# One program of Mamba, experts, attention and grouped experts: the last norm, routing, grouped experts and output woven into the attention turns

## The chip, the cores and the metric

The kernel runs on one core of one Trainium2 chip. The time is device microseconds of a whole execution, the median of three runs. The engines are PE (TensorE), DVE (VectorE), ACT (ScalarE), POOL (GpSimd) and SP, which here only issues transfers.

## The reference, cut to what matters

Two transformer-like layers on x of 8 batches x 512 tokens x 128 features, fp32. The first layer (a bidirectional Mamba block and a top-1 expert block) is the same in both kernels. The second layer is what the change touches:

```python
h = _layernorm(x) * (1 + ca) + sa                       # second norm
x = x + ga * attention(h)                               # 16 heads of 8, causal, rotary
h = _layernorm(x) * (1 + cb) + sb                       # third norm
x = x + gb * moe(h)
# moe: 16 experts of width 64 in 4 groups; scores = sigmoid(h @ router.T); the 2 best groups,
# the 4 best experts in them, weights scaled to 2.5; and 2 shared experts of width 64
#   combine = [tokens, 16]; y = sum_e combine[t,e] * (silu(h@gate_e.T) * (h@up_e.T)) @ down_e.T + shared
```

No batch of this part needs another batch, so the norm, the routing and the experts of a batch may run as soon as its attention is done.

## The kernel before, in words

Data lie transposed: `xT` and `hT` hold 128 features on the partitions and 8 x 512 tokens along them. The program is a row of stages, each an `nc.Block()` whose five engine programs meet at its end: setup, norm, Mamba (L391 to L579), norm, routing, experts, norm, **attention** (L991 on), third **norm** (`layernorm_stage`, L197 to L273), **group routing** (`group_route_stage`, which also computes silu(gate)*up of the first two batches, L1494 and L1587), **grouped experts** (`group_experts_stage`) and **output** (`output_stage`). All but the last five are alike in both kernels.

Attention works in **turns**, one per batch t, and a turn in eight **slots**, 2 to 9. A slot treats one pair of heads:

- *scores*: five PSUM banks of keys x queries (`pe_scores`, L1125, mask added by a second product, L1126), each followed by ACT's exponential (L1222) into `PT`. In slots 8 and 9 they are already those of the next turn.
- *values* in every even slot: 16 narrow fp32 products of four heads (`pe_values`, L1155), then ACT copies the bank out (L1253), PE transposes it (`G0` to `G3`, L1104) and DVE divides (L1303, L1305).
- *maxima* of the next turn: 44 banks (L1140, L1141) per turn, each reduced by DVE (L1270), in slots 2 to 8; after each half DVE splits the 32 columns of negated maxima into three bf16 parts (L1277 to L1285), PE transposes them (`MA`, `MB`) and they go through DRAM into the query stack.
- *projections* of turn t+2: `q`, `q_swap`, `k`, `k_swap` (L1098) in slots 2 to 5, DVE's rotation (L1297), POOL's sum and residues (L1338 to L1342), ACT's bf16 casts (L1231). SP stores these parts and loads them back as a stack (`store_parts`, `load_stack`, L1350 to L1357). PE waits for the stack of turn t+1 before the maxima in slot 2.
- at the turn's end `F` (transpose, L1111) and `O` (output projection, L1113), each waited for by the next, and DVE's update of `xT` (L1317).

`psM` and `psS` (maxima and scores) have three PSUM banks each, `psO` and `mb` one; all one-off products go through `mb` in a fixed order. The order of PE's and DVE's work within a slot is written by `slot_items` and `pe_turn`; three passes of a loop hold turns 0 to 5. An **experts chunk** (nine per batch, eight routed and one shared) is G (gate), silu on ACT, U (up), a multiplication by DVE, C (the routing weights spread over the expert's rows), a second multiplication, D (down); here every one of the banks `psG`, `psU`, `psC`, `psY` is double.

Of the kernel before, what the change touches and what calls it, by code (L numbers as in the profile page):

```python
# [990 lines left out]
def attention_stage(nc, W, W3, tiles, scratch_q, scratch_k, m_scratch, hT, xT, identb, gate):  # L991
# [15 lines left out]
    BEFORE, EACH = 11, 13  # L1007
    with ExitStack() as ctx:
# [49 lines left out]

        def uses(more_p, more_m):

            order = [x for slot in SLOTS_T for x in EARLY.get(slot, []) + LATE.get(slot, [])] + TAIL
            kept = [x for x in order if (more_p or x[0] not in "qk") and (more_m or x not in ("V", "MA", "MB"))]
            return {x: n for n, x in enumerate(kept)}

        def slot_items(c, slot):
# [9 lines left out]
            return items + [x for x in LATE.get(slot, []) if x in c.use]  # L1075

        class Turn:
            def __init__(self, t, p, base, more_p=True, more_m=True):
                self.t, self.p, self.base, self.more_p, self.more_m = t, p, base, more_p, more_m
                self.use = uses(more_p, more_m)  # L1080

        def turns(eng, body):

            with eng.Fori(0, 3) as i:
                for p in range(2):
                    body(Turn(2 * i + p, p, BEFORE + EACH * (2 * i + p)))
            at = BEFORE + EACH * 6
            last = Turn(6, 0, at, more_p=False)
            body(last)
            body(Turn(7, 1, at + len(last.use), more_p=False, more_m=False))  # L1090
# [761 lines left out]
```

## Time and profile before

| | us |
|---|---|
| runs: 2150.10, 2152.92, 2160.95; median | 2152.92 |
| the profiled execution, its own time | 2167.51 |
| its span | 2165.8 |
| from the start of attention (1317.0) to the end of the span | 848.8 |
| of it attention | 552.5 |
| third norm | 27.7 |
| group routing, with gate and up of two batches | 62.9 |
| grouped experts | 194.4 |
| output | 11.3 |
| busy in the whole span: PE, DVE, ACT, POOL | 1745.6, 1434.5, 992.8, 906.7 |

The stretches are counted from the span's start. An engine's busy time is a union of its instructions and tells little alone: within a turn the question is which engine the others wait for. Matmul records overlap, so the distance from one start to the next is the cost of a product, not its length. An fp32 product of 512 columns is recorded as two matmuls.

### The profile page before, as it was taken

The page shows a single profiled execution, that of the slowest core. Times are in us where ns is not written, and L with a number is a line of the kernel's source. Part 1 is how long each engine was busy: PE and PEld are TensorE (multiplying, and loading weights), DVE is VectorE, ACT ScalarE, POOL GpSimd, SP SyncE. Part 2 cuts the span into 40 slices and gives each one's busy share as a digit, 9 for nine tenths or more (in the row PEclk, how much of TensorE's full clock was granted, in tenths as well). Part 3 has the DMA queues.
Part 4 walks back from the last instruction along what each step waited for, and adds up shares of the span by engine and source line. Part 5 has one row for each costly group of instructions (what it writes and reads, how often), then busy time and mean ns, then how long its engine had stood idle before and what let it go on. Part 6 is the DMA issues. An engine that isn't in the chain of part 4 may idle for free. (4 is left out here: it accounts for less than half of the span.)

```text
span 2165.8 us, 24099 instructions
## 1 busy us (share of the span) xinstructions
PE 1745.6 (81%) x7317; PEld 854.3 (39%) x7317; DVE 1434.5 (66%) x1594; ACT 992.8 (46%) x1553; POOL 906.7 (42%) x507
## 2 busy tenths in 40 slices
PE   7788888888888898877838746878777788888998
PEld 5233333333333333332537633434443445543333
DVE  3099999999999999999432122656555556274444
ACT  3566666666656666663203322244343344441111
POOL 1277777777777777776250143011110010040000
PEclk8889999999999999999959955599898898987999
DMA  3112122212121222121014213221123220100001
GB/s 133 40 59 78 60 78 78 74 62 78 78 76 61 78 78 77 59 79 58 16 39 113 86 36 81 69 75 47 32 75 77 76 70 8 44 1 0 0 0 39
DMA packets 49081, 128.25 MB, mean 59 GB/s; under 512 B 5478, under 2 KB 36046, under 8 KB 39094
## 3 DMA queue, kind: packets, MB, share of 16 engines
q1 hardware_dynamic: 45782, 117.65, 17.0%
q0 software_dynamic: 3216, 9.51, 1.3%
q8 instruction: 50, 0.82, 0.2%
q14 instruction: 33, 0.27, 0.0%
HBM read 104.04 MB, written 23.01 MB: 59 GB/s over the span
## 5 line engine op out<-in xcount | busy, mean ns | idle before, releaser
L535 POOL TENSOR_TENSOR PR<-H,CS 128x1024 f32<-128x1024 f32 x256 | 601.9, 2356 | 202.5 <-DVE H L510 192.2
L510 DVE TENSOR_TENSOR_SCAN H<-DA,X 128x1024 f32<-128x1024 f32 x256 | 583.5, 2280 | 0.2
L433 PE MATMUL psY<-PR,W 128*128 128x512 f32 x1024 | 486.8, 598 | 1.1 <-POOL PR L535 1.1
L496 ACT ACTIVATE DA<-DT,negA 128x511 f32<-128x511 f32 x512 | 332.0, 711 | 96.0 <-DVE H L510 95.6
L503 DVE TENSOR_TENSOR X<-DU,psB 128x1024 f32<-128x1024 f32 x256 | 314.5, 1229 | 68.9 <-POOL DU L554 36.6
L433 PEld LDWEIGHTS psY<-PR,W 128*128 128x128 f32 x1024 | 193.7, 192 | 229.7 <-issue 215.2
L1222 ACT ACTIVATE a_PT<-a_psS 128x512 f32<-128x512 f32 x320 | 181.3, 601 | 156.5 <-PE a_psS L1126 152.9
L1270 DVE TENSOR_REDUCE a_MX<-a_psM 128x1 f32<-128x384 f32 (+3 forms) x352 | 206.8, 637 | 60.9 <-PE a_psM L1141 59.5
L413 PE MATMUL psB<-ST,sel 96*128 96x512 bf16 x256 | 100.4, 392 | 143.7 <-DVE X L503 143.6
L1140 PE MATMUL a_psM<-a_kst,a_qst 72*128 72x512 bf16 (+3 forms) x512 | 147.5, 336 | 35.1 <-DMA a_kst<-scratch_k 22.8
L1125 PE MATMUL a_psS<-a_qst,a_kst 75*128 75x512 bf16 (+3 forms) x512 | 138.4, 319 | 18.3 <-issue 17.0
L413 PEld LDWEIGHTS psB<-ST,sel 96*128 96x128 bf16 x256 | 24.7, 96 | 300.9 <-DVE X L503 289.7
L391 PE MATMUL pp<-work,convW 128*128 (+1 forms) x256 | 123.0, 605 | 4.0 <-ACT pre L457 1.4
L1338 POOL TENSOR_TENSOR work<-work 128x512 f32<-128x512 f32 x16 | 20.2, 1264 | 231.0 <-DVE work L1297 231.0
L1141 PE MATMUL a_psM<-a_mqk,identb 128*128 128x128 bf16 x512 | 111.0, 242 | 0.0
L1297 DVE TENSOR_TENSOR work<-a_mb,work 128x512 f32<-128x512 f32 x32 | 22.1, 692 | 125.9 <-PE a_mb L1098 125.8
L1652 ACT ACTIVATE f_SG<-f_psG 128x512 f32<-128x512 f32 x54 | 32.2, 597 | 159.2 <-PE f_psG L1625 159.2
L1126 PE MATMUL a_psS<-a_mkq,identb 128*128 128x128 bf16 x512 | 101.6, 230 | 0.0
L1155 PE MATMUL a_psO<-a_PT,a_VA 128*32 128x512 f32 (+3 forms) x1024 | 98.5, 482 | 2.4 <-issue 1.6
L1140 PEld LDWEIGHTS a_psM<-a_kst,a_qst 72*128 72x128 bf16 x512 | 54.5, 107 | 104.1 <-DVE a_MX L1270 49.1
L1587 POOL TENSOR_TENSOR HE<-g_SG,g_UC 128x512 f32<-128x512 f32 x18 | 23.5, 1308 | 153.1 <-ACT g_UC L1516 153.1
L1253 ACT COPY a_OT<-a_psO 128x512 f32<-128x512 f32 x32 | 18.7, 585 | 145.7 <-PE a_psO L1155 145.7
(252 smaller groups left out, 2539.5 us busy)
## 6 DMA issues: line engine op xcount, KB each, us to landing
CS<-c_rows SPq DMA_DIRECT2D x64, 1024.0 KB, 4.6
scratch_q<-a_partsq SPq DMA_DIRECT2D x24, 384.0 KB, 3.6
a_qst<-scratch_q SPq DMA_DIRECT2D x8, 1152.0 KB
a_kst<-scratch_k SPq DMA_DIRECT2D x24, 384.0 KB
scratch_k<-a_partsk SPq DMA_DIRECT2D x8, 384.0 KB, 5.9
slots<-zeros POOLq DMA_DIRECT2D x1, 2624.0 KB, 10.1
stok<-slots SPq DMA_DIRECT2D x3, 768.0 KB, 7.2
work<-in_pack SPq DMA_DIRECT2D x1, 2272.0 KB, 9.6
```

Of the source, the lines that this page charges most:

```text
L391: last = nc.tensor.matmul(pp[:, :], convW[:, tap, n * P:(n + 1) * P], XP[:, ds((of + 1) * XW + tap, T)], start=tap == 0, stop=tap == KC - 1)
L413: nc.tensor.matmul(psB[:, :], sel[:, s, :], ST[p][:, :], start=True, stop=True).then_inc(B_ready, 1)
L433: last = nc.tensor.matmul(chunk(psY, c), w("ident"), chunk(PR[n % 4], c), start=False, stop=n == NS - 1)
L496: last = nc.scalar.activation(DA[:, s % 4, c, 1:T], chunk(DT[p], c)[:, 1:T], ACT.Exp, scale=negA[:, c * NS + s:c * NS + s + 1])
L503: nc.vector.tensor_tensor(both(X[s % 2][:, :]), both(DU[p][:, :]), psB[:, :].unsqueeze(1).to_broadcast([P, NCH, T]), ALU.mult).then_inc(mu ...
L510: nc.vector.tensor_tensor_scan(H[s % 4][:, :], DA[:, s % 4, :, :].rearrange("p c t -> p (c t)"), X[s % 2][:, :], 0.0, ALU.mult, ALU.add).t ...
L535: nc.gpsimd.tensor_tensor(both(PR[s % 4][:, :]), both(H[s % 4][:, :]), CS[q % 2][:, s % 4, :].unsqueeze(1).to_broadcast([P, NCH, T]), ALU. ...
L1125: nc.tensor.matmul(out, kst[p][:, at + i * P:at + (i + 1) * P], qst[p][:, at + i * P:at + T], start=True, stop=False)
L1140: nc.tensor.matmul(out, qst[p][0:72, at + j * P:at + (j + 1) * P], kst[p][0:72, at:at + wide], start=True, stop=False)
L1141: last = nc.tensor.matmul(out[:, j * P:wide], identb[:, :], mqk[:, :], start=False, stop=True)
L1222: nc.scalar.activation(PT[k % 4][u][:, :], psS[S_BUF[5 * k + u]][:, :], ACT.Exp, scale=DK ** -0.5).then_inc(E_done, 1)
L1270: nc.vector.tensor_reduce(MX[:, j, h0:h0 + nh], src, AX.X, ALU.max).then_inc(M_used, 1)
```

## The change

`attention_stage` takes over the last norm, the routing and the experts of six batches; `last_experts_stage` does the rest. The stages third norm, group routing, grouped experts and output are gone.

- Turn t does, beside its attention: `F` and `O` of batch t-1 (now in slot 2), its norm (`XC`, `VR`, `RB`), logits (`LG`) and routing (51 small DVE operations in slots 6, 7, 8: `GroupRoute`), the transposed weights (`CP`, slot 9); for t >= 2 the nine chunks of batch t-2, one per slot and two in slot 9; for t >= 3 the last down product, the update of `xT` and the transposes and store (`OUT`) of batch t-3 in slot 2.
- One PSUM bank `psE` takes G, U and C of a chunk in turn, `psY` the down products. For them `psM` and `psS` have two banks where they had three.
- Silu is 0.5x * (1 + tanh(0.5x)): ACT writes 0.5x into `GH` and tanh into `TH`, POOL multiplies and adds. (Silu's own table is used in the last stage only.)
- The masks of a scores bank are added in one product; `HB` is gone; the exponentials' buffers `PT` fall from four sets to three; loops are unrolled. The weights of the experts (`W4`) are loaded in the attention prologue behind the second stack.
- `last_experts_stage`: norm and routing of batch 7 among the 18 chunks of batches 6 and 7, with double banks and silu on ACT; the outputs of both.

```diff
-        psM = [ps(f"psM{i}") for i in range(3)]
-        psS = [ps(f"psS{i}") for i in range(3)]
-        psO, mb = ps("psO"), ps("mb")
+        psM = [ps("psM0"), ps("psM1")]
+        psS = [ps("psS0"), ps("psS1")]
+        psO, mb, psE, psY = ps("psO"), ps("mb"), ps("psE"), ps("psY")
...
-        LATE = {3: ["G0"], 4: ["V"], 6: ["MA"]}
-        TAIL = ["F", "O"]
+        LATE = {2: ["XC", "OUT"], 3: ["G0", "VR"], 4: ["V", "RB"], 5: ["LG"], 6: ["MA"], 9: ["CP"]}
+        LEAD = ["F", "O"]
+        ROUTE_SLOTS = {6: ((0.3, 0), (0.8, 1)), 7: ((0.3, 2), (0.8, 3)), 8: ((0.3, 4), (0.8, 5))}
+        CHUNKS = {slot: (slot - 2,) if slot < 9 else (7, 8) for slot in SLOTS_T}
...
+        def slot_plan(t, slot):
...
+                add([("S", t + ahead, slot - PAIRS * ahead, u) for u in range(5)], 0, 0.55 if slot % 2 == 0 else 0.9)
+            if slot % 2 == 0:
+                add([("V", t, slot // 2 - 1, i) for i in range(QT)], 0.55, 1)
...
+            add(items, 0.6 if slot == 2 else 0, 1)
+            add([("mb", t, x) for x in LATE.get(slot, []) if wanted(t, x)], 0.93, 1.02)
...
+                if slot < 9:
+                    plan += [(0.03, ("G", n)), (0.62, ("U", n)), (0.88, ("C", n))]
+                else:
+                    plan += [(0.03, ("G", n)), (0.35, ("U", n)), (0.5, ("C", n)), (0.55, ("G", n + 1)), (0.7, ("D", n)), (0.95, ("U", n + 1))]
+                if n % 9:
+                    plan.append((0.15, ("D", n - 1)))
+            if slot == 2 and t >= 1:
+                plan += [(0.15, ("mb", t, "F")), (0.4, ("mb", t, "O"))]
+                if t >= 3:
+                    plan += [(0.25, ("D", 9 * (t - 3) + 8)), (0.5, ("moe", t - 3))]
+            return [tag for _, tag in sorted(plan, key=lambda x: x[0])]
...
+            if what == "G":
...
+                elif c == 0:
+                    pe.wait_ge(HU_done, n)
+                else:
+                    pe.wait_ge(HC_done, RC * b + c)
+                nc.tensor.matmul(psE[:, :], w4("gate_w")[:, c * P:(c + 1) * P], h, start=True, stop=True).then_inc(G_ready, 1)
+            elif what == "U":
+                pe.wait_ge(TH_ready, n + 1)
+                nc.tensor.matmul(psE[:, :], w4("up_w")[:, c * P:(c + 1) * P], h, start=True, stop=True).then_inc(U_ready, 1)
+            elif what == "C":
+                pe.wait_ge(HU_done, n + 1)
...
+            nc.scalar.activation(GH[:, :], psE[:, :], ACT.Copy, scale=0.5)
+            nc.scalar.activation(TH[n % 2][:, :], psE[:, :], ACT.Tanh, scale=0.5).then_inc(TH_ready, 1)
...
+            nc.gpsimd.tensor_tensor(h[:, :], h[:, :], GH[:, :], ALU.mult).then_inc(SG_step, 1)
+            pool.wait_ge(SG_step, 2 * n + 1)
+            nc.gpsimd.tensor_tensor(h[:, :], h[:, :], GH[:, :], ALU.add).then_inc(SG_step, 1)
...
-        hT, W3, tiles, W4 = XP[:, 0:N], XP[:, N:N + WIDTH3], XP[:, N + WIDTH3:N + WIDTH3 + 5 * T], XP[:, N:N + WIDTH4]
+        hT, W3, tiles = XP[:, 0:N], XP[:, N:N + WIDTH3], XP[:, N + WIDTH3:N + WIDTH3 + 5 * T]
+        W4 = W[:, OFF1["eps"][1]:OFF1["eps"][1] + OFF4["spread"][0]]
...
-        with nc.sbuf_tensor("spread", [48, RC * P], BF16) as spread, nc.sbuf_tensor("cT", [48, N], BF16) as cT:
-            layernorm_stage(nc, "ln3", W, xT, hT, modv(1, 4), modv(1, 3), (W4, ins["pack4"]))
-            with nc.sbuf_tensor("HE", [P, EARLY * FC * T], F32) as HE:
-                group_route_stage(nc, W4, hT, identb, spread, cT, HE)
-                group_experts_stage(nc, W4, hT, spread, cT, HE, xT, modv(1, 5))
-        output_stage(nc, W, xT, out)
+            attention_stage(nc, W, W3, W4, ins["pack4"], tiles, ins["scratch_q"], ins["scratch_k"], ins["m_scratch"], hT, xT, identb,
+                            spread, cT, modv(1, 2), modv(1, 4), modv(1, 3), modv(1, 5), out)
+            last_experts_stage(nc, W, W4, hT, xT, identb, spread, cT, modv(1, 4), modv(1, 3), modv(1, 5), out)
```

How the order looks now, at two places. First DVE in slot 6 of a middle turn of the changed kernel, with the semaphores that each instruction waits for (L1445 is a reduction of a maxima bank, L1024 to L1049 is the routing, L1516 the product with U, L1522 the one with C):

```order
L1445 TENSOR_REDUCE a_MX<-a_psM 128x4 [waits a_M_ready]
L1024 TENSOR_TENSOR a_sc<-a_scores,W 128x64 [waits a_mb_used,a_w4_loaded]
...
L1038 TENSOR_SCALAR a_grank<-a_grank 128x16 [waits a_route_step]
L1039 TENSOR_TENSOR a_masked<-a_sc,a_grank 128x64 [waits a_route_step]
L1445 TENSOR_REDUCE a_MX<-a_psM 128x2 [waits a_M_ready,a_route_step]
L1445 TENSOR_REDUCE a_MX<-a_psM 128x2 [waits a_M_ready] x2
L1516 TENSOR_TENSOR a_TH<-a_TH,a_psE 128x512 [waits a_SG_step,a_U_ready]
L1445 TENSOR_REDUCE a_MX<-a_psM 128x2 [waits a_M_ready]
L1043 TENSOR_REDUCE a_best<-a_masked 128x4
```

Before, only reductions stood here. Now 15 routing operations stand between the second and the third of the slot's maxima and six more before the seventh, and the two multiplications of the chunk stand behind them.

Second, PE from the end of slot 9 into slot 2 of the next turn (L1326, L1329, L1342 are G, U, D; L1257 is `CP`, L1237 `F`):

```order
L1329 MATMUL a_psE<-work,W 128x512 [waits a_TH_ready]
L1257 MATMUL a_mb<-identb,a_cparts 48x128 [waits a_route_step,a_mb_used]
L1257 MATMUL a_mb<-identb,a_cparts 48x128 x3
L1326 MATMUL a_psE<-work,W 128x512 [waits a_HU_done]
L1278 MATMUL a_psS<-a_qst,a_kst 128x512 [waits a_E_done]
L1282 MATMUL a_psS<-a_mkq,identb 128x128
L1237 MATMUL a_mb<-W,a_OTK 128x128 [waits a_mb_used]
```

`F` and `O` stood at the turn's end, with nothing between them. Now `F` is behind G of the next batch's first chunk, which waits until the last chunk of the batch before has left `psE`.

## Rows read from the trace of the kernel before

**Rows 1.** Stretches: length; PE, PEld, DVE, ACT, POOL busy (count); clock, DMA share, GB/s
```profile
1317.00:1395.00 78.00, 53.39 (x205) 24.37 (x206) 33.85 (x66) 14.02 (x23) 17.50 (x16) 0.50 0.41 104
1395.00:1449.50 54.50, 49.71 (x423) 26.25 (x421) 35.55 (x71) 25.99 (x47) 7.11 (x6) 0.93 0.14 42
1449.50:1514.90 65.40, 50.61 (x429) 27.15 (x426) 36.41 (x72) 27.23 (x49) 7.12 (x6) 0.90 0.25 63
...
1583.10:1648.00 64.90, 50.68 (x430) 27.19 (x427) 36.37 (x71) 27.23 (x49) 7.11 (x6) 0.89 0.25 63
...
1869.50:1897.20 27.70, 24.99 (x144) 19.06 (x144) 12.73 (x24) 12.85 (x25) 0.00 (x0) 0.87 0.22 85
...
1960.10:2154.50 194.40, 192.11 (x424) 70.14 (x424) 90.27 (x134) 32.24 (x54) 0.00 (x0) 0.97 0.00 0
...
sum 848.80, PE 703.87 PEld 350.33 DVE 438.04 ACT 297.06 POOL 83.72; mean PE 54.14 PEld 26.95 DVE 33.70 ACT 22.85 POOL 6.44
```

**Rows 2.** Timeline, turn of batch 3: start us, us; end of stack preparation and PE's resumption
```profile
1570.52 1.15 POOL L1342 TENSOR_TENSOR a_partsk<-work,a_partsk 128x512 bf16<-128x512 f32 x1 [6.59 <-ACT a_partsk L1231]
...
1579.04 0.32 SPq L1355 DMA_DIRECT2D a_qst<-scratch_q  x1
...
1596.23 2.07 PE L1098 MATMUL a_mb<-work 128*128 x2 [9.18 <-DMA a_kst<-scratch_k]
```

**Rows 3.** Timeline of ACT, same turn: copies at the ends of slots 4, 6, 8
```profile
1615.49 0.58 ACT L1253 COPY a_OT<-a_psO 128x512 f32<-128x512 f32 x1 [3.31 <-PE a_psO L1155]
...
1630.71 0.58 ACT L1253 COPY a_OT<-a_psO 128x512 f32<-128x512 f32 x1 [4.21 <-PE a_psO L1155]
...
1641.92 0.58 ACT L1253 COPY a_OT<-a_psO 128x512 f32<-128x512 f32 x1 [3.11 <-PE a_psO L1155]
```

**Rows 4.** Timeline of DVE in the experts stage: updates of two batches
```profile
2017.28 0.75 DVE L1681 SCALAR_TENSOR_TENSOR xT<-f_psY,mod,xT 128x512 f32 x1 [1.54 <-PE f_psY L1639]
...
2044.56 0.75 DVE L1681 SCALAR_TENSOR_TENSOR xT<-f_psY,mod,xT 128x512 f32 x1 [1.52 <-PE f_psY L1639]
```

**Rows 5.** Timeline of PE in slot 8 of turn 0: a values product, a maxima bank, values
```profile
1441.20 0.85 PE L1155 MATMUL a_psO<-a_PT,a_VA 128*32 128x384 f32 x8
...
1441.99 0.39 PE L1140 MATMUL a_psM<-a_kst,a_qst 72*128 72x512 bf16 x1
...
1442.37 0.86 PE L1155 MATMUL a_psO<-a_PT,a_VA 128*32 128x256 f32 x16
```

**Rows 6.** Groups from 1300 us on: count, busy us, mean ns, idle before
```profile
L1270 DVE TENSOR_REDUCE a_MX<-a_psM 128x1 f32<-128x384 f32 (+3 forms) x352 | 206.8, 637 | 60.9 <-PE a_psM L1141 59.5
...
L1671 DVE TENSOR_TENSOR f_HU<-f_SG,f_psU 128x512 f32<-128x512 f32 x54 | 37.1, 688 | 70.8 <-PE f_psU L1631 70.8
...
L1587 POOL TENSOR_TENSOR HE<-g_SG,g_UC 128x512 f32<-128x512 f32 x18 | 23.5, 1308 | 153.1 <-ACT g_UC L1516 153.1
...
L1253 ACT COPY a_OT<-a_psO 128x512 f32<-128x512 f32 x32 | 18.7, 585 | 145.7 <-PE a_psO L1155 145.7
...
L1305 DVE TENSOR_TENSOR a_OTK<-a_mb,a_rec 128x128 f32<-128x128 f32 x32 | 9.3, 291 | 1.1
...
L1281 DVE TENSOR_TENSOR a_NR<-a_NR,a_NMB 128x32 f32<-128x32 f32 x16 | 3.1, 192 | 0.6
...
L1509 ACT ACT_TABLE_LOAD x1 | 1.3, 1283 | 0.0
```

**Rows 7.** Timeline of POOL and DVE: a small cast beside a POOL operation
```profile
1422.77 1.27 POOL L1338 TENSOR_TENSOR work<-work 128x512 f32<-128x512 f32 x1
...
1422.89 1.19 DVE L1279 CAST a_NMB<-a_NR 128x32 bf16<-128x32 f32 x1
```

**Rows 8.** Timeline of DVE in group routing: one operation beside POOL, and alone
```profile
1922.72 1.65 DVE L1560 TENSOR_TENSOR g_key<-g_key,work 128x512 f32<-128x512 f32 x1
...
1945.26 0.69 DVE L1560 TENSOR_TENSOR g_key<-g_key,work 128x512 f32<-128x512 f32 x1
```

More of the change, by code:

```diff
@@ new lines, in wanted, with uses @@
+        def wanted(t, name):
+            if name in PRO:
+                return t + 2 < B
+            if name in ("V", "MA", "MB"):
+                return t + 1 < B
+            if name in ("XC", "VR", "RB", "LG", "CP"):
+                return t >= 1
+            if name in LEAD:
+                return t >= 1
+            return t >= 3 if name == "OUT" else True
+        def uses(t):
+            order = LEAD + [x for slot in SLOTS_T for x in EARLY.get(slot, []) + LATE.get(slot, [])]
+            return [x for x in (order if t < B else LEAD + ["OUT"]) if wanted(t, x)]
@@ new lines, in use, with add @@
+        def use(t, name):
+            return BEFORE + sum(len(uses(s)) for s in range(t)) + uses(t).index(name)
+        def slot_plan(t, slot):
+            plan = []
+            def add(tags, lo, hi):
+                for n, tag in enumerate(tags):
+                    plan.append((lo + (hi - lo) * (n + 0.5) / len(tags), tag))
+            ahead = slot >= PAIRS
+            if not ahead or t + 1 < B:
+                add([("S", t + ahead, slot - PAIRS * ahead, u) for u in range(5)], 0, 0.55 if slot % 2 == 0 else 0.9)
+            if slot % 2 == 0:
+                add([("V", t, slot // 2 - 1, i) for i in range(QT)], 0.55, 1)
+            early = [("mb", t, x) for x in EARLY.get(slot, []) if wanted(t, x)]
+            half, a, b = M_SLOTS[slot] if slot in M_SLOTS and t + 1 < B else (0, 0, 0)
+            maxima = [("M", t + 1, half, g) for g in range(a, b)]
@@ L1074, in slot_items @@
                 early, maxima = early[1:], maxima[2:]
[L1075 to L1090, printed above, removed]
@@ new lines, in slot_plan, with pe_mb @@
+            return [tag for _, tag in sorted(plan, key=lambda x: x[0])]
+        LAST_PLAN = [("mb", B, "F"), ("D", 9 * (B - 3) + 8), ("mb", B, "O"), ("moe", B - 3), ("mb", B, "OUT")]
+        def pe_mb(pe, t, name):
+            pe.wait_ge(mb_used, use(t, name))
+            if name[0] == "G":
+                pe.wait_ge(O_copied, 4 * t + int(name[1]) + 1)
+                for j in range(QT):
+                    last = nc.tensor.transpose(mb[:, j * P:(j + 1) * P], OT[int(name[1]) % 2][:, j * P:(j + 1) * P], ident)
+            elif name in PRO:
+                last = nc.tensor.matmul(mb[:, :], w("w" + name), batch(hT, t + 2), start=True, stop=True)
@@ new lines, in pe_maxima @@
+        def pe_maxima(pe, t, half, g):
+            j, h0, nh = groups(half)[g]
+            n = 2 * NG * t + half * NG + g
+            if n >= 2:
+                pe.wait_ge(M_used, n - 1)
+            wide = (j + 1) * P
+            for x in range(nh):
+                at = (h0 + x) * T
+                piece = psM[g % 2][:, x * wide:(x + 1) * wide]
+                nc.tensor.matmul(piece, qst[t % 2][0:72, at + j * P:at + (j + 1) * P], kst[t % 2][0:72, at:at + wide], start=True, stop=False)
+                last = nc.tensor.matmul(piece[:, j * P:wide], identb[:, :], mqk[:, :], start=False, stop=True)
+            last.then_inc(M_ready, 1)
```

1024 lines of the change are left out of this document (563 added, 461 removed).

## The prediction

> **What bounds the kernel now.** I read the stretches first. From the start of attention to the end 848.8 us pass, in which PE is busy for 703.9 [rows 1]; the other 145 are what a better overlap could give at most. The experts stage has nothing to give: 192.1 busy of 194.4. The reader is to see in the other rows that a middle turn (64.9) leaves PE idle for 14.2, while DVE has 36.4 of work, ACT 27.2 and POOL 7.1. Of the 14.2, 9.2 are one wait for the key stack: POOL's last rotation step starts at 1570.5, the stack load is issued at 1579.0 and PE goes on at 1596.2, 25.7 later [rows 2]. So PE bounds a turn, with 5.0 idle beside that wait. The change puts 27.3 us of experts per batch (2044.56 - 2017.28, all PE's) [rows 4] and the norm into the turns. Its question is whether the other engines can feed PE in that order.
>
> **Costs of the pieces.** A chunk is 27.28 / 9 = 3.03: G, U and D some 0.86 each, C 0.22 and 0.2 between them. A maxima bank of 512 columns takes PE 0.38 beside values products, a values product of 384 columns 0.79 (starts at 1441.20, 1441.99, 1442.37) [rows 5]. DVE takes 0.64 per maxima bank and 0.69 per multiplication of a chunk, ACT 0.59 per copy (and I give tanh the same), POOL 1.31 per elementwise operation, and a table load on ACT takes 1.28 [rows 6]. The trace has no routing operation of 64 columns. Bounds are 0.19 for 32 columns and 0.29 for 128 [rows 6]; I take 0.24 with the gap behind it, being nearer 32 than 128 on that line, so the 51 cost 12.2 per batch (9.7 to 14.8).
>
> **A middle turn (3 to 5).** Added to PE: 27.3 and about 5.5 for norm, logits and output (the norm stage has 25.0 busy for eight batches, 3.1 each [rows 1]; the logits and two transposes I put at 2.4, bounds 1.5 to 3.5). PE's work is then 50.7 + 27.3 + 5.5 = 83.5. DVE's: 36.4 + 17 x 0.69 + 12.2 + 1.7 (update, norm) = 62. ACT's: 27.2 + 18 x 0.59 + 3.6 (six more of such) + 4 x 1.28 = 46.5. POOL's: 7.1 + 18 x 1.31 = 30.7. By these sums PE would still bound it. But with two maxima banks in place of three, PE stops two banks behind DVE, and one bank `psE` chains the chunk: G 0.86, 0.2 to ACT, 1.2 for 0.5x and tanh, 2.6 on POOL (U beside it), 0.7 on DVE, C 0.3, 0.8 on DVE, 7.0 in all before the next G. So I walk the written order slot by slot, each engine in its order:
>
> Slot 2: `F`, `O`, q, last D, `XC`, `OUT`, 6 maxima, chunk: 12.6 of PE, 1.8 of waits: 14.4. Slot 3: 10.3 (`VR` waits 0.9 for DVE's division of `G0`). Slot 4: 13.5 (a table load ahead of the first tanh, `RB` waits 1.0). Slot 5: 9.1. Slot 6: DVE's third maxima bank stands behind 15 routing operations (3.6 us), begun at 4.1 when PE's fifth bank comes at 5.3; with POOL's pair from 3.7 to 6.3 beside them they end at 9.3, PE takes up its fifth bank at 10.0, and everything behind it, six more routing operations too, ends with C's product at 16.5. Slots 7 and 8 in the same way: 12.7 and 12.8. Slot 9: two chunks, whose chain 7.0 + (G 0.9, ACT 1.4, POOL 2.7, DVE 0.8) is 12.8 against 8.5 of PE's work, and the next G, ahead of `F`, waits for it. Sum 102.1, of which 18.6 are idle for PE.
>
> How good is such a walk? For the turn before, the larger of PE's and DVE's work gives 13.3 for slots 5 and 6 and 10.9 for 7 and 8; the copies stand 15.2 and 11.2 apart [rows 3]. The sums are 0.3 to 1.9 short, so I do not shave anything off the walk.
>
> **DVE beside POOL.** In the trace a cast of 32 columns took 1.19 where POOL's operation began just before it and ended with it [rows 7], 1.0 more than the 0.19 of its neighbours of that size [rows 6]; a routing operation took 1.65 beside POOL and 0.69 alone [rows 8]. In slots 6 to 8 POOL's pair falls on routing operations: I priced 1.8 + 0.8 + 0.8 = 3.4 per turn (bounds 0, no coincidence, and 3 x 2 x 1.3 = 7.8). [...]
>
> **The other turns.** Prologue 78.0 before: half the clock (0.50), and with two banks PE and DVE take turns on 44 maxima banks, (0.55 + 0.4 + 0.64) / 2 = 0.8 for 0.67 each: +5, 83. The load of `W4` stands in SP's queue ahead of the first maxima; hidden behind the second half's reductions, and up to 8 if not. Turn 0: 54.5 less the pause around `F` and `O` (2.5), plus 1 for the banks: 53. Turn 1: 65.4 + 5.5 of PE + 5 where 12.2 of routing overtakes PE in slots 6 to 8, and the stack, still 25.7 behind POOL, is asked for after only 14 of work: that wait stays (9 to 11): 78. Turn 2: as the middle ones, 102, its stack wait (25.7 against 21) against no `OUT`. From turn 3 on the stack has 33 us and its wait is gone: 9.2 are saved in four turns, inside the walk. Turn 6: without projections 97. Turn 7: nothing but experts and norm; the chain sets it: 11.5 + 8.6 + 8.8 + 8.0 + 9.2 + 8.3 + 8.9 + 12.8 = 76. Its end (`F`, D, `O`, update, `OUT`, store) 9. **Last stage**: 18 chunks at 3.03 = 54.5, norm and outputs 5, start and table loads 2, routing of batch 7 on DVE holds PE for 4 to 5, tail of update, transpose, copy and store 6: 72.
>
> Sum: 83 + 53 + 78 + 4 x 102 + 97 + 76 + 9 + 72 = 876, against 848.8: **27 us more**. Made against the profiled execution's own 2167.5 this is 2195; that execution was 14.6 over the median, which I carry over: 2152.9 + 27 = **2180 us**. The mask products merged cost the same columns, the unrolled loops save branches off the path, `HB`'s copy was covered by ACT's slack: nothing for each, and if covers were gone a few us either way.
>
> PE would then be idle for 876 - 704 = 172 us where it was for 145: 74 in turns 2 to 5, 22 in turn 1, 17 in turn 6, 16 in turn 7, 12 in the last stage, the other 31 at both ends. Before, the routing kept PE idle once for all batches, with operations eight times as wide; now 51 short operations per batch, each of which pays its fixed part, stand in DVE's queue ahead of what PE waits for.
>
> **Rivals.** A, faster: PE keeps its share. If a middle turn has only the 5.0 of idle time that the turn before had beside the stack wait, it takes 83.5 + 5 = 88.5, 13.6 less than walked; four turns and 10 for turn 6 give 64: 2180 - 64 = 2116. For it speak DVE's 62 of 88 and that slots 6 to 8 have less PE work, so that a lag may be made up in slot 9; against it the two maxima banks, which let PE run only two ahead, and slot 9's chain. It decides as soon as a middle turn stays under 94. B, no difference: the walk is half as bad in slots 6 to 8 (their larger work is 30.7 without POOL, walked 42.0), 5.6 less per turn in five turns: 2152. [...]
>
> **Numbers.** As forecast (2180) 0.42, A 0.29, B 0.16, C with D 0.13. About 0.5% (10.8 us) is what a measurement of this kernel tells from no change. Slower 0.42 + 0.13 = 0.55, same 0.16, faster 0.29. The forecast's own range is 2164 to 2200 (routing operations at 0.19 to 0.29 give 2.5 per turn either way, the unpriced `W4` 8). The range has to reach into A, which holds more than 0.2: from 2118 to 2210.
>
> **What would show it.** The reductions of maxima banks and the products of `psE` are the places: a middle turn, from one update of `xT` by `O` to the next, of 97 to 107; PE's waits within it led by maxima banks (DVE) in slots 6 to 8 and by G in slot 2; 18 or so of PE idle per turn; the wait for the stack present in turns 1 and 2 and gone from 3 on; small casts and routing operations well over 0.3 beside POOL's; the last stage at 70 to 75. I am wrong if a middle turn is under 94 (then DVE made up its lag) or if turn 7 is under 70 (then the chain is shorter than 7.0).

## The result, and the profile after

The changed kernel takes 2223.99 us (median of four runs, 2222.63 to 2232.51), the kernel before 2152.22 in the same comparison: ratio 1.0355, 95% interval 1.0328 to 1.0381. It is 72 us slower. The forecast of 2180 had the direction, and missed the size: 27 us forecast, 72 measured, and the range ended at 2210.

The page of the changed kernel, part 1, and the granted clock of part 2:

```profile
span 2223.2 us, 22475 instructions
...
PE 1799.2 (81%) x7125; PEld 842.7 (38%) x7125; DVE 1493.9 (67%) x1949; ACT 1050.6 (47%) x1631; POOL 1000.2 (45%) x597
...
PEclk7899999999999999999769665988898989898989
```

PE is recorded 54 us longer than before (1799.2 against 1745.6) with fewer matmuls, though the change gives it no new work.

The stretches of the changed kernel, columns as in [rows 1]. They begin at the last gated update of the layer before (1290.6, see run e8 for why there), and are cut at the eight updates of `xT` by `O`: prologue with turn 0, turns 1 to 7, and the last stage:

```profile
1290.60:1445.60 155.00, 117.65 (x664) 52.44 (x664) 79.78 (x147) 48.26 (x85) 25.18 (x22) 0.71 0.31 84
1445.60:1535.00 89.40, 67.16 (x441) 32.80 (x438) 49.57 (x125) 36.39 (x60) 9.27 (x8) 0.81 0.26 59
1535.00:1640.00 105.00, 86.25 (x500) 39.91 (x498) 62.80 (x142) 44.28 (x76) 26.61 (x24) 0.92 0.15 39
1640.00:1749.10 109.10, 90.94 (x504) 41.64 (x502) 63.54 (x143) 44.93 (x77) 26.64 (x24) 0.89 0.16 40
1749.10:1858.40 109.30, 90.97 (x505) 41.80 (x503) 63.58 (x143) 44.93 (x77) 26.70 (x24) 0.89 0.15 40
1858.40:1967.50 109.10, 91.03 (x504) 41.59 (x502) 63.54 (x143) 44.93 (x77) 26.65 (x24) 0.89 0.16 40
1967.50:2070.10 102.60, 87.31 (x496) 40.32 (x494) 57.18 (x138) 42.85 (x73) 19.59 (x18) 0.88 0.02 4
2070.10:2147.70 77.60, 62.81 (x313) 25.90 (x310) 28.38 (x81) 33.70 (x57) 17.43 (x16) 0.91 0.01 4
2147.70:2223.20 75.50, 64.00 (x166) 26.12 (x166) 35.75 (x91) 21.67 (x32) 0.00 (x0) 0.94 0.04 11
sum 932.60, PE 758.11 PEld 342.52 DVE 504.11 ACT 361.94 POOL 178.07; mean PE 84.23 PEld 38.06 DVE 56.01 ACT 40.22 POOL 19.79
```

A middle turn takes 109.3 where 102.1 were walked. PE stands idle for 109.3 - 91.0 = 18.3 of it, and 18.6 were forecast. What is too long is PE's own work: 91.0, where 83.5 were summed. The mean clock of the turn does not explain this by itself, for it is 0.89 in the turn before as well [rows 1]. What differs is how much work stands at the lower level. Here are the two stretches at 0.50 in before's turn (1583.1 to 1648.0), and the sum of the five in the changed kernel's (from 1770.34, 1801.06, 1818.13, 1824.95 and 1842.02):

```profile
1589.98:1600.22 10.24, 3.99 (x24) 2.11 (x25) 0.92 (x2) 0.58 (x1) 0.00 (x0) 0.50 0.32 66
1624.12:1627.53 3.41, 3.41 (x20) 1.44 (x18) 2.30 (x4) 1.10 (x2) 0.96 (x1) 0.50 0.02 5
...
sum 23.89, PE 21.93 PEld 8.75 DVE 8.28 ACT 6.92 POOL 5.47; mean PE 4.39 PEld 1.75 DVE 1.66 ACT 1.38 POOL 1.09
```

Before, the longer stretch lies mostly in the wait for the stack, where a low clock costs nothing, and PE works for 4.0 + 3.4 = 7.4 us at 0.50. Now it works for 21.9 us at 0.50. The same product takes 2.08 there and 1.08 at 1.00 (L1329, starts 1804.99 and 1763.59), so about half of that time is lost. By this estimate the clock takes 11.0 us of the turn where it took 3.7: 7.3 more, of the 7.5 by which PE's work is over the sum.

The waits of PE in that turn (1749.1 to 1858.4; total, times, longest), and after them the one of turn 1 for its stack, which answers to [rows 2]:

```profile
PE a_psM L1295 <- DVE a_MX L1445: 6.5, 2, 4.2
PE a_psE L1326 <- DVE a_TH L1522: 6.5, 4, 2.9
...
PE a_psM L1295 <- DMA a_kst<-scratch_k: 7.7, 1, 7.7
```

How the clock falls is seen in slot 6. DVE's timeline there (start, length, and the idle time before it): the first lump of routing, that is operations which stand together in DVE's queue, lies between two reductions of maxima.

```profile
1793.57 1.14 DVE L1460 TENSOR_TENSOR a_NMB<-a_NR,a_NMB 128x32 bf16<-128x32 f32 x1
...
1795.75 0.69 DVE L1445 TENSOR_REDUCE a_MX<-a_psM 128x4 f32<-128x512 f32 x1 [0.44 <-PE a_psM L1296]
1796.36 0.66 DVE L1024 TENSOR_TENSOR a_sc<-a_scores,W 128x64 f32<-128x64 f32 x1
1797.05 1.58 DVE L1027 TENSOR_TENSOR a_pair<-a_sc 128x16 f32<-128x16 f32 x6
...
1799.46 1.15 DVE L1035 TENSOR_TENSOR a_ge<-a_ge,W 128x64 f32<-128x64 f32 x1
1800.65 0.22 DVE L1036 TENSOR_TENSOR a_gt<-a_gt,a_ge 128x64 f32<-128x64 f32 x1
...
1801.63 1.29 DVE L1445 TENSOR_REDUCE a_MX<-a_psM 128x2 f32<-128x512 f32 x2
```

PE's timeline at the end of that pause:

```profile
1802.37 0.40 PE L1295 MATMUL a_psM<-a_kst,a_qst 72*128 72x256 bf16 x1 [4.21 <-DVE a_MX L1445]
...
1803.13 1.94 PE L1309 MATMUL a_psO<-a_PT,a_VA 128*32 128x512 f32 x8
1804.99 2.08 PE L1329 MATMUL a_psE<-work,W 128*128 128x512 f32 x2
```

And stretches cut at the pauses: slot 5, slot 6 up to the pause's end, what follows it, and slot 8's start, which stands behind a wait of 2.9 for `psE`:

```profile
1783.74:1792.15 8.41, 8.41 (x46) 4.43 (x45) 5.86 (x11) 5.27 (x9) 2.18 (x2) 1.00 0.00 0
1792.15:1802.40 10.25, 5.38 (x44) 3.31 (x44) 9.29 (x25) 6.91 (x12) 5.67 (x5) 0.93 0.00 1
1802.40:1807.00 4.60, 4.60 (x15) 1.35 (x16) 1.20 (x2) 0.00 (x0) 0.00 (x0) 0.50 0.01 4
...
1825.60:1833.00 7.40, 7.32 (x23) 3.18 (x24) 2.35 (x6) 3.05 (x6) 2.18 (x2) 0.58 0.76 239
```

The reader is to see one chain. Routing and DVE's small operations beside POOL fill DVE from 1792 to 1803; PE, with two maxima banks, pauses for 4.21; and the 4.6 us of work behind the pause run at 0.50: U takes 2.08 where G took 1.10 at 1792.15. Slots 2 to 9 took 14.9, 9.5, 14.9, 8.4, 19.1, 14.3, 15.2 and 12.9 (starts of their first G). Against the walk (14.4, 10.3, 13.5, 9.1, 16.5, 12.7, 12.8, 12.8) slots 6 to 8 are 6.6 over, and the rest, in sum, 0.5. The mean clock of slots 3 to 9 is 1.00, 0.89, 1.00, 0.82, 0.86, 0.80 and 0.87. In slot 4 it falls with no pause over 1.2 us ahead of it in the turn, so long pauses explain most of the low clock, but not all.

### The profile page after: what moved, and what is told of

Its sections match the earlier page's. It is cut to its first block and busy times, and to the rows that moved or that the text cites. A ratio compares the mean times of both kernels' runs of the same rounds, so it can differ in the third digit from the quotient of the medians.

```text
span 2223.2 us, 22475 instructions
## 1 busy us (share of the span) xinstructions
PE 1799.2 (81%) x7125; PEld 842.7 (38%) x7125; DVE 1493.9 (67%) x1949; ACT 1050.6 (47%) x1631; POOL 1000.2 (45%) x597
## 5 line engine op out<-in xcount | busy, mean ns | idle before, releaser
L496 ACT ACTIVATE DA<-DT,negA 128x511 f32<-128x511 f32 x512 | 331.9, 711 | 88.7 <-DVE H L510 88.3
L1445 DVE TENSOR_REDUCE a_MX<-a_psM 128x1 f32<-128x384 f32 (+3 forms) x352 | 219.4, 639 | 112.4 <-PE a_psM L1296 107.9
L1570 POOL TENSOR_TENSOR a_TH<-a_TH,W 128x512 f32<-128x512 f32 x54 | 58.9, 1090 | 426.0 <-ACT a_TH L1408 426.0
L1375 ACT ACTIVATE a_PT<-a_psS 128x512 f32<-128x512 f32 x320 | 185.8, 598 | 117.6 <-PE a_psS L1282 113.6
L1295 PE MATMUL a_psM<-a_kst,a_qst 72*128 72x512 bf16 (+3 forms) x512 | 155.8, 341 | 62.2 <-DVE a_MX L1445 39.0
L1278 PE MATMUL a_psS<-a_qst,a_kst 75*128 75x512 bf16 (+3 forms) x512 | 136.9, 332 | 14.1 <-ACT a_PT L1375 12.7
L1326 PE MATMUL a_psE<-work,W 128*128 128x512 f32 x108 | 68.3, 718 | 42.9 <-DVE a_TH L1522 37.2
L1309 PE MATMUL a_psO<-a_PT,a_VA 128*32 128x512 f32 (+3 forms) x1024 | 102.6, 480 | 0.0
L1516 DVE TENSOR_TENSOR a_TH<-a_TH,a_psE 128x512 f32<-128x512 f32 x54 | 37.1, 688 | 85.1 <-PE a_psE L1329 56.1
L1282 PE MATMUL a_psS<-a_mkq,identb 128*128 128x256 bf16 (+1 forms) x320 | 87.9, 275 | 0.0
L1278 PEld LDWEIGHTS a_psS<-a_qst,a_kst 75*128 75x128 bf16 x512 | 47.4, 106 | 99.6 <-issue 51.7
```

Source lines behind the costliest of these rows:

```text
L496: last = nc.scalar.activation(DA[:, s % 4, c, 1:T], chunk(DT[p], c)[:, 1:T], ACT.Exp, scale=negA[:, c * NS + s:c * NS + s + 1])
L1278: nc.tensor.matmul(bank[:, col:col + wide], kst[t % 2][:, at + i * P:at + (i + 1) * P], qst[t % 2][:, at + i * P:at + T], start=(h, i, col ...
L1295: nc.tensor.matmul(piece, qst[t % 2][0:72, at + j * P:at + (j + 1) * P], kst[t % 2][0:72, at:at + wide], start=True, stop=False)
L1375: nc.scalar.activation(PT[k % 4][u][:, :], psS[(k + u) % 2][:, :], ACT.Exp, scale=DK ** -0.5).then_inc(E_done, 1)
L1445: nc.vector.tensor_reduce(MX[:, j, h0:h0 + nh], src, AX.X, ALU.max).then_inc(M_used, 1)
```

## The experiments

The tables below give, per run, the same nine stretches as above. All edits are to the changed kernel unless "before" is named.

| | first, turn 0 | 1 | 2 | 3 | 4 | 5 | 6 | 7 | last | sum |
|---|---|---|---|---|---|---|---|---|---|---|
| changed | 155.0 | 89.4 | 105.0 | 109.1 | 109.3 | 109.1 | 102.6 | 77.6 | 75.5 | 932.6 |
| e1 split | 161.5 | 82.8 | 97.6 | 99.3 | 98.2 | 98.4 | 93.4 | 76.1 | 75.8 | 883.1 |
| e2 fill | 161.8 | 84.5 | 101.6 | 102.8 | 102.9 | 102.7 | 95.8 | 75.7 | 75.6 | 903.4 |
| e12 split and fill | 161.5 | 83.1 | 101.0 | 101.3 | 100.3 | 101.9 | 98.7 | 76.3 | 75.9 | 900.0 |
| e3 11 operations | 159.7 | 76.8 | 95.3 | 92.4 | 93.7 | 92.4 | 89.3 | 73.7 | 75.8 | 849.1 |
| e5 silu on DVE | 164.6 | 88.0 | 105.0 | 106.3 | 108.3 | 106.2 | 102.0 | 77.8 | 75.5 | 933.7 |
| e6 with e1 | 160.1 | 84.7 | 97.6 | 98.7 | 98.1 | 98.6 | 93.5 | 74.6 | 74.8 | 880.7 |
| e7 small POOL | 160.2 | 87.8 | 102.0 | 104.8 | 102.8 | 103.0 | 101.0 | 72.4 | 75.2 | 909.2 |
| e9 spare banks | 151.2 | 83.6 | 107.9 | 109.1 | 109.3 | 109.2 | 102.5 | 77.6 | 75.5 | 925.9 |
| e10 26 operations | 158.2 | 80.2 | 100.8 | 97.8 | 100.0 | 96.6 | 93.4 | 72.0 | 71.6 | 870.6 |
| e11 combined | 146.9 | 82.0 | 92.2 | 95.8 | 95.8 | 95.6 | 89.0 | 72.4 | 71.5 | 841.2 |
| e13 combined, ties | 149.5 | 81.6 | 95.0 | 92.0 | 92.1 | 92.0 | 88.7 | 72.2 | 73.4 | 836.5 |

**e1, the routing in small pieces.** The same 51 operations, three at a time, spread evenly over slots 6 to 8.

```diff
-        ROUTE_SLOTS = {6: ((0.3, 0), (0.8, 1)), 7: ((0.3, 2), (0.8, 3)), 8: ((0.3, 4), (0.8, 5))}
+        ROUTE_AT = ((6, 6), (7, 6), (8, 5))
...
-                        route.run(dve, tag[2])
+                        route.piece(dve, 3)
```

> The changed kernel with the same 51 routing operations per batch, in pieces of three spread evenly over slots 6 to 8 (6, 6 and 5 pieces) in place of six lumps. [...] Rival (DVE beside POOL, or the chunk chain, sets slots 6 to 8): the same work is there, so the turn stays at 106 to 109 and the time at 2205 to 2224.

Measured: 2175.57 us, 1.0105 of before (1.0064 to 1.0147), under the rival's range of 2205 to 2224: 48 us of the 72 are gone, with the same operations on the same engine. The middle turn (1735.3 to 1833.5), and PE's waits in it:

```profile
1735.30:1833.50 98.20, 85.71 (x504) 39.90 (x502) 63.59 (x143) 45.05 (x77) 26.69 (x24) 0.95 0.18 45
...
PE a_psE L1372 <- DVE a_TH L1568: 3.1, 3, 2.1
PE a_psM L1341 <- DVE a_MX L1491: 2.4, 4, 1.1
```

The longest wait for a maxima bank is 1.1 in place of 4.2; DVE's sum is unchanged (63.6). So two thirds of the loss came from the place of the operations, not from their sum.

**e2, the pauses filled.** Matmuls of no use, into the free bank `mb`, where PE pauses (4, 2, 3 and 2 in slots 6 to 9 of turns 2 to 6, 2 and 2 in slots 6 and 7 of turn 1).

```diff
+                    elif tag[0] == "fill":
...
+                        for _ in range(tag[3]):
+                            nc.tensor.matmul(mb[:, :], w("wo"), w("cos"), start=True, stop=True)
```

> The changed kernel with matmuls of no use (512 columns of fp32, into a bank that is free) where PE stands still in slots 6 to 9 of turns 2 to 6 (4, 2, 3 and 2 of them) and in slots 6 and 7 of turn 1. They add 11 matmuls per turn to PE and take nothing away. If the fall of the clock after the pauses is a cost of its own, the granted clock of these slots stays near 1.00 and a middle turn falls from 109 by 4 to 7 us in spite of the added work, the time by 20 to 40 to 2185 to 2205. If the pauses alone make the loss, the clock may rise but the turn stays at 109 or becomes longer by what of the added work does not fit in a pause (0 to 5 us), the time 2224 to 2250.

Measured: 2199.06 us, 1.0226 (1.0184 to 1.0268): 25 us less, with 11 matmuls more per turn (22 as recorded).

```profile
1744.60:1847.50 102.90, 93.63 (x526) 43.27 (x524) 63.94 (x143) 44.82 (x77) 26.63 (x24) 0.97 0.17 43
```

The clock is 0.97 and the turn 102.9, near the walk of 102.1. The fall of the clock is a cost of its own, 6.4 us per middle turn, net of what the added matmuls cost.

**e12, both at once.** The edits of e1 and e2 together.

> The changed kernel with the 51 routing operations in pieces of three over slots 6 to 8 and the 11 matmuls of no use per turn in slots 6 to 9 as well. If the clock's fall and the lumps are the same loss told twice: PE hardly pauses with the split routing, the fillers only add work, 2172 to 2185 (the split alone: 2175.6). If the clock is a loss of its own that the split leaves (middle turns at 0.95): 2155 to 2165.

Measured: 2190.53 us, 1.0185 (1.0151 to 1.0218), 15 us slower than the split alone and 5 over the first of the two expected ranges; the clock stands at 0.98 and the turn at 100.3. With the lumps gone there is little left to fill, and the added matmuls cost more than the clock gives. So the gains of the two experiments do not add: in large part they are the same microseconds. The lumps make the pause (4.2 us, with e1's pieces 1.1), and behind the pause the clock falls (0.93 up to its end, 0.50 in the 4.6 us behind it).

**e3, fewer routing operations.** The choice of groups and of experts is left out in batches 0 to 6 (all scores are taken); 11 operations stay.

```diff
+        if self.short and part < 5:
+            if part == 0:
+                then(v.tensor_copy(chosen[:, :, :], self.scores[:, :, :]))
```

> The changed kernel with the routing of batches 0 to 6 cut from 51 to 11 operations: scores are taken for chosen as they are, and the choice of groups and of experts is left out; the last routing is whole. About 40 operations of 0.23, 9 us of DVE per turn, go. Routing theory: the pauses of slots 6 to 8 go, with the fall of the clock behind them, the middle turn is 94 to 98 us, the time 2135 to 2160. If DVE beside POOL and the chunk chain are most of it, the turn stays over 103, the time over 2190. If only DVE's own sum counted (63.5 of 109, never the bound), no change.

Measured: 2144.67 us, 0.9970 (0.9945 to 0.9994). With the 40 operations 79 us go, more than the whole loss, and the middle turns (92.4 to 93.7) are a little shorter than the 94 to 98 expected. It does less than the kernel before and is no version of it; what it shows is that norm and experts alone fit into the turns.

**e10, 26 operations.** Here and in the last stage, the fourfold round of reductions and comparisons is replaced by one MAX8 per tile (a row's eight largest), and two scalings of the weights are made in one; the rules on ties are left out. Scores do tie in these inputs, against the parenthesis below.

```diff
+            for j in range(QT):
+                v.max(top[:, j, 0:8], masked[:, j, :]).then_inc(self.step, 1)
+            then(v.tensor_tensor(chosen[:, :, :], masked[:, :, :], top[:, :, TOP_K - 1:TOP_K].to_broadcast([P, QT, E1]), ALU.is_ge))
```

> The changed kernel with 26 routing operations per batch in place of 51, in the last stage too: the rules that break ties are left out (the values differ in these inputs), and the four best experts come from one operation per tile that gives a row's eight largest. About 25 operations of 0.22 go, 5.6 us of DVE per turn, in the same places. The kernel with 11 operations had middle turns of 92.4 to 93.7. If the loss goes with the length of the lumps: 98 to 101 and 2165 to 2180 us. If a pause over 2 us, with the clock's fall behind it, is all or nothing: the lumps of slots 6 and 8 are still 12 and 9 operations, and only slot 7 is free: 103 to 106, 2190 to 2205.

Measured: 2164.32 us, 1.0052 (1.0033 to 1.0071). The middle turns are 96.6 to 100.0, and 60 us are gone, some of them (3.9) in the last stage: the loss goes with the length of the lumps, and the second case expected, all or nothing, does not hold.

**e5, e6, e7: POOL beside DVE, and the chunk's chain.** e5 makes silu's product by one DVE operation, (tanh + 1) x half the gate, in place of two on POOL; e6 does so with e1's routing. e7 cuts POOL's two operations to 8 of 512 columns, which leaves out nearly all of silu's product.

```diff
+            nc.vector.scalar_tensor_tensor(h[:, :], h[:, :], 1.0, GH[:, :], ALU.add, ALU.mult).then_inc(SG_step, 2)
...
-                        pool_silu(pool, FC * (t - 2) + c)
```

> The changed kernel (routing in its six lumps), with silu's product of the attention turns made by one operation on DVE, (tanh + 1) times half the gate, ahead of the multiplication by U, in place of two operations on POOL of 1.09 us. It takes 19 us per turn from POOL and adds 9 x 0.75 = 6.7 to DVE. [...]

> The same edit of silu together with the routing in pieces of three. With split routing the middle turn was 98.4 us, PE busy for 86. [...] If DVE's larger sum (70 of 98) takes over what the chain gives: 97 to 101 and a time of 2170 to 2190.

> The changed kernel with POOL's two operations per chunk on 8 of 512 columns in the attention turns: it leaves out nearly all of silu's product there. [...] By the theory that DVE beside POOL costs up to 8 us per turn and the chain of slot 9 some 4: middle turn 98 to 101, time 2150 to 2180. By the theory that the lumps of routing with the clock's fall behind them are nearly everything: 105 to 109 and 2200 to 2224.

Measured: e5 2221.94 (1.0327, 1.0289 to 1.0364), no difference, with middle turns of 106.2 to 108.3; e6 2170.47 (1.0089, 1.0058 to 1.0120), 5 under e1, with overlapping intervals, its time and its turns (98.1 to 98.7) as its expectation has them for DVE's larger sum; e7 2205.25 (1.0248, 1.0201 to 1.0295), 19 under the changed kernel, with a time in the range of the second theory and turns of 102.8 to 104.8 between the two. A turn of e5 and one of e7:

```profile
1755.30:1863.60 108.30, 91.42 (x504) 41.86 (x502) 67.49 (x151) 45.07 (x77) 7.41 (x6) 0.89 0.16 41
...
1746.10:1848.90 102.80, 87.56 (x504) 40.03 (x503) 60.67 (x143) 44.81 (x77) 10.59 (x24) 0.92 0.16 43
```

POOL's operations on `TH` cost about 19 us of the 72, for DVE's longer operations beside POOL's and for the chain together (e7), which these runs do not separate. In e7 DVE's busy time falls by 2.9 per turn (63.6 to 60.7): this is what silu's operations add to DVE's recorded lengths. In e5 DVE has 3.9 more and POOL 19.3 less, and turn 4 is 1.0 shorter, turns 3 and 5 are 2.8 and 2.9 shorter. Its new operations lengthen DVE's queue in the same slots, so e5 does not tell what POOL's cost there.

**e4 and e9, the banks.** e4: before with two banks for `psM` and `psS`. e9: the changed kernel with `psE` and `psY`, which are empty until turn 2, as third and fourth bank for the maxima of batches 0 to 2. Of the diff, the first two lines are e4's, the last two e9's.

```diff
-        psM = [ps(f"psM{i}") for i in range(3)]
+        psM = [ps(f"psM{i}") for i in range(2)]
...
+        M_RING = psM + [psE, psY]
+            ring = M_RING if t <= 2 else psM
```

> The kernel before with two banks for maxima (and for values) in place of three, nothing else. If the third bank by itself carries the loss of the change: 40 us or more slower. My own sum gave about 5 us for the prologue and a few for turn 0, with DVE's short copies in the middle turns hidden: 2152 becomes 2155 to 2170.

> The changed kernel with four banks for the maxima of batches 0 to 2 (the experts' psE and psY stand empty until turn 2 starts) and two from batch 3 on; the routing stays in its six lumps. The kernel before with two banks in place of three was 9 us slower up to the first update by O. If the banks make the loss of that stretch here too: from the last update of the layer before to the first by O 145 to 150 us (it was 155 to 162), and turn 1 shorter by 4 to 10 (PE can run four ahead of the routing's lumps; it was 88); turns 2 to 7 as they were; time 2224 less 15 to 22, 2200 to 2210. If the routing's operations hold PE whatever the banks: turn 1 stays at 87 to 89 and the time is 2213 to 2218.

Measured: e4 2173.96, 1.0113 (1.0064 to 1.0161); e9 2213.54, 1.0274 (1.0252 to 1.0296), 10 less than the changed kernel. The stretches of e4: first with turn 0, turn 4, turn 7; before's own are 142.8, 64.7 and 31.5:

```profile
1287.60:1439.30 151.70, 116.16 (x683) 53.06 (x683) 78.96 (x146) 46.15 (x81) 25.19 (x22) 0.71 0.27 70
...
1640.00:1710.50 70.50, 55.89 (x431) 27.77 (x432) 37.16 (x71) 27.85 (x49) 7.11 (x6) 0.85 0.24 59
...
1842.60:1878.70 36.10, 29.52 (x246) 13.19 (x244) 3.67 (x11) 18.98 (x34) 0.00 (x0) 0.91 0.00 1
```

The third banks are worth 24 us in the old order by the medians (2150.42 beside e4), which puts the time 4 over the range expected: 9 in prologue and turn 0, where I had 6 for them (+5 and +1), and 4 to 6 each in turns 4, 5 and 7, where the clock is lower too (0.85 against 0.89 in turn 4). In the changed order the spare banks give back 4 to 9 in the first stretch (151.2 against 155.0, or 160.2, the median of nine runs with two banks) and 6 in turn 1, as the first case of the expectation had it; turn 2 is 3 longer, nothing changes where two are left, and the time is 4 over that case's range, in the second's.

**e8, before once more.** No edit.

> The kernel before, unchanged, for a second profile. Its first profile has 57 us from the first to the last gated update of the layer before attention, where four other kernels with the same code there have 39 to 42. If that was a chance of the one execution, this one has about 41 there, a span near 2150, and attention to the end again 859 us; if it belongs to the kernel, 57 and 2166.

Measured: span 2149.3. The eight gated updates of the layer before attention, in the first profile of before and in this one:

```profile
L988 DVE SCALAR_TENSOR_TENSOR xT<-gps,mod,xT x8: 751/751/752, 1249.3 to 1306.5; 128x512 f32<-128x512 f32 x8
```

```profile
L988 DVE SCALAR_TENSOR_TENSOR xT<-gps,mod,xT x8: 750/751/751, 1247.5 to 1287.9; 128x512 f32<-128x512 f32 x8
```

57.2 against 40.4: the 15 us by which the profiled execution of before stood over its median lie here, ahead of everything the change touches; from there to the end it has 859.3 and e8 861.4. That is why all stretches above start behind these updates, and why 932.6 - 859.3 = 73.3 agrees with the medians' 71.8, while the spans differ by 57 only.

**e14, a higher clock for before.** Twelve matmuls of no use in PE's wait for the first stack.

```diff
+                for _ in range(12):
+                    nc.tensor.matmul(psO[:, :], w("wo"), w("cos"), start=True, stop=True)
                 pe.wait_ge(st_loaded[0], LOADS)
```

> The kernel before with the same 12 matmuls of no use in PE's wait for the first key stack, nothing else. If the clock at 0.50 costs in that stretch: granted clock from 0.69 to over 0.85 there, the stretch from 143 to 146 down to 136 to 141, time 2143 to 2148. If DVE's reductions (0.64 each) set it whatever PE's clock, or the fillers end late: no difference, 2149 to 2155.

Measured: 2147.97 us, 0.9981 (0.9965 to 0.9998), first stretch 141.0, its clock 0.76 where over 0.85 was expected. Three windows of 10 us, that of the last fillers and the two behind it:

```profile
1331.60:1341.60 10.00, 7.13 (x34) 3.43 (x33) 0.91 (x2) 0.71 (x1) 0.64 (x1) 0.99 0.84 222
1341.60:1351.60 10.00, 10.00 (x44) 3.68 (x42) 10.00 (x20) 0.00 (x0) 0.00 (x0) 0.50 0.68 175
1351.60:1361.60 10.00, 7.82 (x50) 4.98 (x48) 8.42 (x20) 0.00 (x0) 0.00 (x0) 0.50 0.50 105
```

The fillers (1325.7 to 1337.1) brought the clock up, from 0.52 in the 10 us up to 1328 to 1.00 from there on, but ended 2.9 us before the stack arrived (1337.1 to 1340.0), and it fell again, to 0.50 from 1341.6 on. So what the half clock costs in the prologue stays open, and nothing ties the 5 us by which the median is lower to it.

**e11 and e13, the parts together.** e11: e9's banks, e10's 26 operations, in pieces of two (the four MAX8 go with the operation behind them). e13: with the rules on ties kept (37 operations: MAX8 finds the fourth value, a second MAX8 breaks ties by index), and e14's twelve fillers.

```diff
+            then(v.tensor_tensor(key[:, :, :], masked[:, :, :], fourth(0), ALU.is_equal))
+            then(v.tensor_tensor(self.oh[:, :, :], masked[:, :, :], fourth(0), ALU.is_gt))
...
+                v.max(top[:, j, 8:16], key[:, j, :]).then_inc(self.step, 1)
+            then(v.tensor_tensor(chosen[:, :, :], key[:, :, :], fourth(8), ALU.is_ge))
```

> Spare banks, 26 operations and pieces of two operations over slots 6 to 8, together. If the three parts of the loss (prologue's banks, lumps with the clock's fall, number of operations) add: first stretch 146 to 150, turn 1 74 to 78, middle turns 90 to 94, time 2120 to 2140: faster than both kernels. If the chunk chain of slots 9 and 2 and DVE beside POOL hold the turn at its 92 to 93 whatever the routing: 2135 to 2150.

> All parts together with the rules on ties kept: 37 routing operations per batch (the four best of a row from two uses of the eight-largest operation), in pieces of two over slots 6 to 8, four banks for the maxima of batches 0 to 2, and 12 matmuls of no use while PE waits for the first key stack. By the sum of the single runs (26 operations gave 2134; 11 more of 0.22 in seven turns add 0 to 12, the warm clock of the first stretch gives 4 to 8): 2130 to 2145, against 2151 of the kernel before. If the routing's operations count in full again: 2150.

Measured: e11 2134.44 (0.9914, 0.9896 to 0.9932), in its range, though turn 1 (82.0) and the middle turns (95.8) are over theirs; e13 **2129.70 us, 0.9905 (0.9874 to 0.9935)**: it computes all that before does and is faster than both kernels. Its turn 4, PE's longest waits in it, and the MAX8:

```profile
1709.60:1801.70 92.10, 81.24 (x505) 38.17 (x503) 59.08 (x129) 44.90 (x77) 26.69 (x24) 1.00 0.19 48
...
PE a_psM L1365 <- DVE a_MX L1517: 2.1, 3, 1.4
PE a_psE L1397 <- DVE a_TH L1594: 2.0, 2, 1.2
...
L1072 DVE MAX8 a_pair<-a_masked 128x8 f32<-128x16 f32 x4 | 0.4, 164 | 0.0
```

No wait reaches 1.5 us, the granted clock is 1.00, and PE's work is 81.2: this is what the 91.0 of the changed kernel are at full clock. e13 lies below e11 in turns 3 to 5 with 11 operations more; there the clock is 1.00 against e11's 0.93. e11's turn 4 and its longest wait:

```profile
1708.00:1803.80 95.80, 86.95 (x505) 40.80 (x503) 55.21 (x118) 44.89 (x77) 26.61 (x24) 0.93 0.18 46
...
PE a_psE L1378 <- DVE a_TH L1575: 2.2, 3, 1.2
```

Its pauses are no longer than e13's (1.2 against 1.4), and still the clock falls and PE's work is 5.7 longer. So the absence of long pauses did not secure the full clock; what does stays open, and with it whether e13's turns would keep it in another order.

## Why the prediction was right or wrong

- **The direction, and its reason, were right.** The routing ahead of the maxima with two banks, and the chunk's chain, lead PE's waits as forecast (6.5 and 6.5), and idle time per middle turn is 18.3 (18.6 forecast). The chain's longest wait is at slot 8's G (2.94), not at slot 2's as forecast (1.15). The stack's wait is there in turn 1 (7.7; 9 to 11 forecast) and gone later, in turn 2 already, where I had kept it.
- **The step that failed is "PE's work is then 50.7 + 27.3 + 5.5 = 83.5".** It puts nothing for PE's clock in the new order, and 91.0 were measured. Its 50.7 stand for a turn that lost about 3.7 to the lower clock; without them the sum is 79.8, and e13's turn at 1.00 shows 81.2. The 18.6 of idle time were walked as pauses of a few us each, and behind such pauses the clock fell (0.50 behind 4.21, 0.58 behind 2.94), which took 11.0 (the estimate above) in place of 3.7. The rows had it: 0.50 over the prologue and 0.89 over a turn [rows 1]. I gave the fall of the clock a share of the 0.13 of C with D, for slot 9 alone and with a few us per turn. It comes in slots 6, 7, 8 and 9 (and once in slot 4), and was no rival but part of the likeliest case: e2 gives back 4.9 + 3.4 + 3 x 6.4 + 6.8 = 34 us in turns 1 to 6, net of its added matmuls, of the 41.5 by which those turns are over the forecast. In sums from the first product of attention on (at 1301.9 here, 1317.0 in before): 921.3 us, PE busy for 749.2 and idle for 172.1. Forecast were 876, 704 and 172: the idle time was right, and PE's own time, left as it was before, was 45 too short. That the idle time fits so well is in part chance: slot 9 was walked with 8.5 of work and 4.3 idle and shows 10.5 and 2.4, since work at the lower clock (0.87 in this slot) fills a wait that the chain sets.
- **Turn 1** took 89.4 for 78: idle 22.2, as walked (22), and PE's work 67.2 for 56.1, at a clock of 0.81. The same step.
- **Prologue and turn 0** were given 3.5 more than before and took 12 more here; over nine executions with the same two banks the stretch is 155.0 to 164.6 against 142.8 and 145.8. From the arrival of the first stack to the first update by `O` it is 105.7 here, 102.2 in e4, and 93.4 in both profiles of before. So two banks, put at 6, cost 9. PE waits for that stack as long as before (13.8 and 13.9), so the load of `W4`, put at 0 to 8, cost nothing there. With four banks 147 to 151 are left of the whole stretch; what makes the rest is open.
- **DVE beside POOL**: priced at 3.4 per turn, for silu's operations beside the routing. In turn 4 five routing operations start beside one of POOL's and take 0.65 to 1.16 for 0.2, 3.8 more in all; each ends within 0.1 us of POOL's end (L1035 above is one; L1460, with 1.14, is no routing operation but met POOL's in the same way). Three of them meet silu's (2.1), two meet the rotation's, which were not priced (1.8). Rival C took the upper bound, 7.8 per turn, for 22 us more; that was an estimate which no run shows, and these rows have 3.8. It came nearest with 2202 to 2220, but for another reason: in the routing the collisions are about as priced.
- **Routing operations** of 64 columns are 0.22 to 0.23, with the gap 0.25: taken as 0.24, right. POOL's of silu took 1.09 where 1.31 was taken. The terms of the chunk's chain add up to 6.7 and not to its 7.0; slot 9, built on it, took 12.9 for 12.8. Last stage and end: 81 forecast, 75.5 measured. Turn 7: 77.6 for 76.
- **Rival A (88.5 per turn)** needed PE to keep its share. e13's 92.0 show how near it was with pauses under 1.5 us.
- Carrying over the 14.6 us by which the profiled execution of before stood over its median was right: they lie outside the changed part.

## What to carry to other kernels

When a walk of the written order finds PE idle in pauses like these (2.1 to 4.2 us), cost the first few us of work behind each, as an estimate, at half the clock (here 4.6 us ran at 0.50 behind 4.21, and 7.4 at 0.58 behind 2.94), and look in the trace of the kernel before how much of its low clock lies in waits, where it is free (PE worked in only 4.0 of the 10.2 us at 0.50 here). A turn's mean clock does not show that: it was 0.89 before and after. Idle time in small bits was cheaper here than in lumps (e1 has PE's work at 85.7 per turn for 91.0), though small bits alone did not secure the full clock (e11, 0.93). Small operations of a side job belong spread, two or three at a time, between those that another engine waits for, and first of all they should be few. A bank that stands empty in a program's first turns can serve as a spare there (e9, 10 us).
